# Turning k in VectorE's 32x32 blocks and through memory, not on TensorE, in an attention kernel on Trainium2

## The chip, the cores and the metric

The kernel runs on one core of one Trainium2 chip. The metric is the device time of one execution, in microseconds (us). Below, PE is TensorE (its weight loads have a row of their own, PEld), DVE is VectorE, ACT is ScalarE, POOL is GpSimd, and SP is SyncE, which issues all the DMAs of this kernel.

## The reference, cut to what matters

```python
x = x + attn(layernorm(x))          # x: 4 x 512 x 512; 32 query heads, 8 k/v heads, D = 128, chunks of 128 tokens
x = x + ffn(layernorm(x))

# attn, for each k/v head and batch; chunk n of four
q, k = rope(q), rope(k)
G = cumsum(g)                                                   # within a chunk
y_intra = ((q @ k.T) * causal(exp(G_i - G_j))) @ (v * dt)
cstates = einsum('jd,je->de', k * exp(G_last - G), v * dt)      # needs k with tokens on the rows
state   = state * exp(G_last) + cstates                         # over the chunks
y_inter = (q * exp(G)) @ state_before
y = rms_norm(y_intra + y_inter) * gnorm_w
y = y * (gate * sigmoid(gate))                                  # gate = x @ Wg.T
return y @ Wo.T
```

## The kernel before

Three stages follow one another: the first norm with v and the tables (to about 135 us of the trace), the attention stage (to about 1290 us), and the output projection with the second norm and the expert layer.

The attention stage is a sequence of 32 steps, one for each group `g` of four query heads (8) and each batch `b` (4), numbered `n = 4g + b`. Each step works through four chunks `c` of 128 tokens. Most groups run inside a hardware loop on each engine except PE, whose code is written out. Within a step PE does, in this order, for the chunks: `scores` (q times k, three passes over high and low parts), projections of the next step's k and q and of this step's gates (`next_unit`, `gates`; 12 matmuls each), `chunk_state` (the product `cstates`, three passes, into `p_cst`) for chunks 0 to 2, and `mix` (y from the state and from the probabilities). Nine projections share three PSUM banks in turn, so that a projection can begin only when VectorE has read what stood in its bank.

Each engine runs its own instructions in order, and semaphores join them. On VectorE the order in a step is: probabilities, scaled q, low part of the next chunk's q, `make_z` of the chunk before, a rope rotation (three instructions at L104 to L106), `turn_z` (z's 32x32 blocks), `make_state` (which empties `p_cst`, L972 and L975), `make_gate`. The rope's last addition is POOL's (L114).

The product `cstates` wants k with its tokens on the partitions, while the projection and the scores leave k with its head dimension there. `k_turn` therefore has PE transpose three chunks of the next step's k into PSUM bank `p_tok` (L805), between the last gate projection and `mix` of chunk 3. ACT copies `p_tok` rounded to the high part (`save_k`, L1120), VectorE takes the low part (`k_tok_low`, L929), and `chunk_state` of chunk 0 in the next step waits for both, and for `xw_low` of POOL (L1228).

Once in four steps weights are split too. In steps with b = 2 (of the groups 0 to 6) VectorE and POOL each take half of the low part of the next group's q weights (`q_low_weights`, L905, and `w_low`, L1241), just ahead of the step's end; in steps with b = 3 VectorE takes half of the gate weights' low part (L910) at the end, and POOL the other half at the start of the following step.

`make_tanh` (ACT, L1095) writes tanh of the gate's projection into a tile `tanh`, and waits until the gate before it has been made out of that tile; `make_gate` (VectorE, L935) makes `gate[c % 2]` of it.

SP issues, in a step: v for the next step, rows of the tables `g` and `e` (`load_g`, L663; `load_e`, L667), weights (L650, L657), and the stores of z (`store_z`, L752, four DMAs, for half 0 at c = 2 and for half 1 at c = 0 of the following step). The row of g for the next step's chunk 0 is issued at c = 1. POOL masks it (L1214) after it has copied a small table (L1206); both stand in POOL's queue ahead of the last rope addition.

## Time and profile before

| | |
|---|---|
| median of 3 runs | 1774.86 us (1773.87 to 1774.93) |
| the profiled execution's own time | 1773.33 us |
| its span, first to last instruction | 1771.5 us |
| mean granted TensorE clock | 0.996 |
| one attention step (four of them: 36.00, 35.90, 35.90, 35.90 us) | 35.9 us |
| PE, VectorE, ScalarE, GpSimd busy, share of the span | 98%, 72%, 40%, 48% |

The table's busy shares are averages over three stages. In the attention stage VectorE is far busier than its average, and PE is busy all the time. A busy PE says only that some matmul was under way by the trace's model; how closely they follow one another is read from their start times.

### The profile page before, as it was taken

The numbers are of one execution on the slowest core, as the hardware profiler recorded it, in microseconds if no ns is written. First come the engines' busy times: TensorE is split into PE (matmuls) and PEld (weight loads), VectorE is DVE, ScalarE is ACT, GpSimd is POOL, SyncE is SP. The second block draws the span as 40 slices with busy tenths as digits, with TensorE's granted clock in tenths as the row PEclk, the third lists the DMA queues.
The fourth block names the chain that finished last, engine by engine and source line by source line (L and its number), as shares of the span: only waits on it lengthen the run. The fifth ranks groups of instructions, "written<-read, shape, count | busy, mean of one in ns | idle before, by whom it ended". The sixth has DMA issues, their size and how long they took to land. (4 is left out here: it accounts for less than half of the span.)

```text
span 1771.5 us, 27984 instructions
## 1 busy us (share of the span) xinstructions
PE 1741.7 (98%) x8744; PEld 1469.5 (83%) x8744; DVE 1270.9 (72%) x2353; ACT 715.5 (40%) x2232; POOL 851.4 (48%) x862
## 2 busy tenths in 40 slices
PE   7998999999999999999999999999989999999998
PEld 6787888888888888888888888888878888888886
DVE  5326898988999999999898999998874333333332
ACT  3424444454445444544445444544652111111111
POOL 3225677667757766676766775776501101010101
PEclk9999999999999999999999999999999999999999
DMA  6333323423333333343342333333572323232321
GB/s 203 91 106 100 115 87 99 127 91 107 119 90 114 121 89 96 106 122 87 99 128 93 104 118 92 111 93 111 191 248 79 107 72 107 72 106 72 106 72 47
DMA packets 145985, 190.31 MB, mean 107 GB/s; under 512 B 9136, under 2 KB 79792, under 8 KB 145840
## 3 DMA queue, kind: packets, MB, share of 16 engines
q1 hardware_dynamic: 145840, 188.58, 34.8%
q8 instruction: 66, 1.08, 0.3%
q14 instruction: 79, 0.65, 0.1%
HBM read 141.89 MB, written 46.66 MB: 106 GB/s over the span
## 5 line engine op out<-in xcount | busy, mean ns | idle before, releaser
L114 POOL TENSOR_TENSOR q<-raw_wo_early 128x512 f32<-128x512 f32 x128 | 164.9, 1289 | 202.0 <-DVE raw_wo_early L106 201.5
L85 PE MATMUL p_proj<-shared,wq_hi 128*128 128x512 f32 x744 | 244.5, 390 | 0.0
L1113 ACT ACTIVATE square<-p_y 128x128 f32<-128x128 f32 x512 | 134.6, 278 | 216.4 <-PE p_y L837 216.0
L1846 POOL TENSOR_TENSOR var<-mv,eps 128x1 f32<-128x1 f32 x16 | 3.1, 192 | 403.9 <-DVE mv L1696 403.9
L837 PE MATMUL p_y<-v_tok,probs 128*128 128x128 f32 x1024 | 182.1, 275 | 0.0
L985 DVE SCALAR_TENSOR_TENSOR z<-p_y,srstd,gate 128x128 f32<-128x128 f32 x512 | 143.4, 341 | 48.9 <-issue 31.8
L1088 ACT ACTIVATE probs<-g_row,stab 128x128 f32<-128x128 f32 x512 | 164.3, 406 | 25.2 <-POOL g_row L1214 25.2
L85 PE MATMUL p_kept<-wg_hi,shared 128*128 128x512 f32 x560 | 173.2, 390 | 0.0
L1228 POOL TENSOR_TENSOR xw_lo<-xw_raw,xw_hi 128x512 fp32r<-128x512 f32 x96 | 131.1, 1365 | 86.6 <-ACT xw_hi L1125 86.6
L85 PEld LDWEIGHTS p_proj<-shared,wq_hi 128*128 128x128 f32 x744 | 139.6, 188 | 30.4 <-DVE raw_wo_early L106 1.2
L85 PE MATMUL p_proj<-wg_hi,shared 128*128 128x512 f32 x528 | 162.6, 389 | 0.0
L1236 POOL TENSOR_TENSOR srstd<-svar,mhalf 128x4 f32<-128x4 f32 x128 | 157.8, 1232 | 10.0
L837 PEld LDWEIGHTS p_y<-v_tok,probs 128*128 128x128 f32 x1024 | 150.0, 192 | 2.5
L836 PE MATMUL p_y<-state,qs 128*128 128x128 f32 x768 | 148.3, 275 | 1.4 <-DVE qs L950 1.4
L85 PE MATMUL p_proj<-shared,wq_lo 128*128 128x512 f32 x372 | 144.8, 389 | 0.0
L1378 DVE TENSOR_TENSOR wq_lo<-w_raw,wq_hi 128x1024 fp32r<-128x1024 f32 x62 | 75.8, 1223 | 84.3 <-ACT wq_hi L1373 84.3
L836 PEld LDWEIGHTS p_y<-state,qs 128*128 128x128 f32 x768 | 121.1, 191 | 7.1 <-issue 2.2
L1125 ACT ACTIVATE xw_hi<-xw_raw 128x512 fp32r<-128x512 f32 x96 | 60.7, 632 | 155.2 <-POOL xw_raw L1224 129.7
L85 PEld LDWEIGHTS p_kept<-wg_hi,shared 128*128 128x128 f32 x560 | 104.6, 188 | 21.5
L85 PEld LDWEIGHTS p_proj<-wg_hi,shared 128*128 128x128 f32 x528 | 99.1, 188 | 20.9
L1224 POOL TENSOR_TENSOR xw_raw<-v_tok,stab 128x512 f32<-128x512 f32 x96 | 111.3, 1159 | 0.1
L85 PE MATMUL p_kept<-wg_lo,shared 128*128 128x512 f32 x280 | 109.2, 390 | 0.0
(239 smaller groups left out, 4402.2 us busy)
## 6 DMA issues: line engine op xcount, KB each, us to landing
g_row<-g_scratch SPq DMA_DIRECT2D x128, 256.0 KB, 4.9
z_scratch<-z_st SPq DMA_DIRECT2D x256, 128.0 KB
w_raw<-z_scratch SPq DMA_DIRECT2D x62, 512.0 KB, 6.5
e_row<-e_scratch SPq DMA_DIRECT2D x96, 256.0 KB, 4.0
w_raw<-in_wq_t SPq DMA_DIRECT2D x16, 512.0 KB, 7.2
w_raw<-in_wg_t SPq DMA_DIRECT2D x16, 512.0 KB, 5.3
v_tok<-v_scratch SPq DMA_DIRECT2D x32, 256.0 KB, 2.9
v_scratch<-n_xin SPq DMA_DIRECT2D x22, 256.0 KB, 2.3
```

Source lines behind the costliest of these rows:

```text
L85: mm = pe.matmul(out, lhs[a], rhs[e], start=(i == 0 and j == 0), stop=(i == len(pairs) - 1 and j == 2))
L114: pool.tensor_tensor(out, keep["rope_a"][:, s, :], keep["rope_b"][:, s, :], ALU.add).then_inc(keep["roped"], 1)
L836: pe.matmul(p_y[c % 2][:, h, :], qs[:, h, :], state[:, c % 2, h, :], start=True, stop=False)
L837: mm = pe.matmul(p_y[c % 2][:, h, :], probs[:, c % 2, h, :], v_tok[:, b % 2, c, :], start=(c == 0), stop=True)
L985: zz = dve.scalar_tensor_tensor(z[:, h, :], p_y[c % 2][:, h, :], srstd[:, c, h:h + 1], gate[:, c % 2, h * D:(h + 1) * D], ALU.mult, ALU.mult)
L1088: e = act.activation(probs[:, c % 2, h, :], g_row[:, c % 2, h, :], ACT.Exp, bias=stab[:, b % 2, c, T_BIAS, h:h + 1])
L1113: s = act.activation(square[:, h, :], p_y[c % 2][:, h, :], ACT.Square, scale=2.0 / float(np.sqrt(D)), accum_out=ssum[:, c, h:h + 1])
L1125: act.activation(xw[0][:, :, :], xw_raw[:, :, :], ACT.Copy).then_inc(xw_hi_set, 1)
L1224: pool.tensor_tensor(xw_raw[:, :, :], v, w, ALU.mult).then_inc(xw_raw_set, 1)
L1228: pool.tensor_tensor(xw[1][:, :, :], xw_raw[:, :, :], xw[0][:, :, :].bitcast(F32), ALU.subtract).then_inc(xw_set, 1)
L1236: pool.tensor_tensor(srstd[:, c, :], svar[:, c, :], mhalf[:, :], ALU.pow).then_inc(srstd_set, 1)
L1378: dve.tensor_tensor(by_half(keep["z_lo"][slot]), raw_z(keep, raw_slot), by_half(keep["z_hi"][slot].bitcast(F32)), ALU.subtract).then_inc(k ...
```

## The change

Three things change in the attention stage; the other edits (one semaphore in the place of two or three, in the first and the last stage) leave instructions and waits as they were.

1. PE turns k only for the first step. For each later one VectorE transposes the 32x32 blocks of k in place of order (`turn_k`), after `turn_z` of chunk 0; SP stores them to memory in four DMAs (`store_k`, one for each 32 partitions), each block at its turned place, and loads them back (`load_turned`) with the tokens on the partitions, ahead of z's stores. High and low part are then made of this SBUF tile `k_turned`.
2. `k_tok_low` thus reads two SBUF tiles, where it read one of PSUM and one of SBUF.
3. tanh is written into the place of the gate that is made of it, and waits for z of two chunks before, not for the last gate.

```diff
+            def store_k(n):
+                sp.wait_ge(k_blocks_set, n)
+                for a in range(P // BL):
+                    sp.dma_start(k_dram.rearrange("c (b j) d -> j (c b) d", j=BL)[:, :, a * BL:(a + 1) * BL],
+                                 k_blocks[a * BL:(a + 1) * BL].rearrange("j c b i -> j (c b) i")).then_inc(k_out, 16)
+            def load_turned(n):
+                sp.wait_ge(k_out, 16 * (P // BL) * n)
+                sp.dma_start(k_turned[:, :, :], k_dram.rearrange("c t d -> t c d")).then_inc(k_in, 16)
@@ sync, step
                         load_e(g, b, 3)
+                        if ahead(n):
+                            store_k(n + 1)
                     elif c == 2 and ahead(n):
+                        load_turned(n + 1)
                         sp.wait_ge(state_set, 3 * n + 3)
@@ tensor
-            def k_turn(n, b):
-                pe.wait_ge(roped, ROPED * n + 1)
-                wait_ge(pe, tok_saved, n)
+            def first_k_turn():
+                pe.wait_ge(roped, 1)
                 for c in range(NC - 1):
-                    t = pe.transpose(p_tok[:, c, :], k[:, b % 2, c * C:(c + 1) * C], ident[:, :])
+                    t = pe.transpose(p_tok[:, c, :], k[:, 0, c * C:(c + 1) * C], ident[:, :])
                 t.then_inc(tok_done, 1)
@@ tensor, step
                 gates(g, b, n, 3)
-                k_turn(n + 1, b + 1)
                 mix(g, b, n, 3)
@@ vector
-                dve.tensor_tensor(k_tok[1][:, :, :], p_tok[:, 0:NC - 1, :], k_tok[0][:, :, :].bitcast(F32),
+                dve.tensor_tensor(k_tok[1][:, :, :], by_tokens(n), k_tok[0][:, :, :].bitcast(F32),
                                   ALU.subtract).then_inc(tok_saved, 1)
+            def turn_k(n, b):
+                dve.wait_ge(roped, ROPED * n + 1)
+                wait_ge(dve, k_out, 16 * (P // BL) * (n - 1))
+                dve.transpose(k_blocks[:, :, :, :], k[:, b % 2, 0:(NC - 1) * C].rearrange("p (c b i) -> p c b i", c=NC - 1, i=BL)
+                              ).then_inc(k_blocks_set, 1)
@@ vector, make_gate
-                dve.scalar_tensor_tensor(gate[:, c % 2, :], tanh[:, :], 1.0,
+                dve.scalar_tensor_tensor(gate[:, c % 2, :], gate[:, c % 2, :], 1.0,
@@ vector, step
                 turn_z(n, 0)
+                turn_k(n + 1, b + 1)
                 make_state(n, b, 1)
@@ scalar, make_tanh
-                wait_ge(act, gate_set, NC * n + c)
+                wait_ge(act, z_set, NC * n + c - 1)
@@ scalar
-            def save_k(n):
-                act.wait_ge(tok_done, n + 1)
+            def k_tok_high(n):
+                if has_last(n):
+                    act.wait_ge(k_in, 16 * n)
+                else:
+                    act.wait_ge(tok_done, 1)
                 wait_ge(act, cst_done, 3 * n)
-                act.activation(k_tok[0][:, :, :], p_tok[:, 0:NC - 1, :], ACT.Copy).then_inc(tok_hi_set, 1)
+                act.activation(k_tok[0][:, :, :], by_tokens(n), ACT.Copy).then_inc(tok_hi_set, 1)
```

`by_tokens(n)` is `k_turned` for all steps but the first, and `p_tok` for that.

On PE, at the end of a step (the last gate projection into `p_kept`, then `mix` of chunk 3), the rows before:

```order
 L85 MATMUL p_kept<-wg_hi,shared 128x512 x2
 L85 MATMUL p_kept<-wg_lo,shared 128x512
 L805 MATMUL p_tok<-ident,k 128x128 x3
 L836 MATMUL p_y<-state,qs 128x128
 L837 MATMUL p_y<-v_tok,probs 128x128
```

and after:

```order
 L85 MATMUL p_kept<-wg_hi,shared 128x512 x2
 L85 MATMUL p_kept<-wg_lo,shared 128x512
 L857 MATMUL p_y<-state,qs 128x128
 L858 MATMUL p_y<-v_tok,probs 128x128
```

The three transposes have gone from between them.

On VectorE, in the middle of a step (rope of the next step's second q head, z's blocks of chunk 0, the state of chunk 1, the gate of chunk 1), before:

```order
 L106 TENSOR_TENSOR raw_wo_early<-p_proj,raw_wo_early 64x512
 L994 STREAM_TRANSPOSE z_st<-z 128x16x32
 L975 SCALAR_TENSOR_TENSOR state<-state,e_row,p_cst 128x128 x4
 L935 SCALAR_TENSOR_TENSOR gate<-tanh,p_proj 128x512
 L943 TENSOR_TENSOR probs<-p_score,probs 128x512
```

and after:

```order
 L106 TENSOR_TENSOR raw_wo_early<-p_proj,raw_wo_early 64x512
 L1019 STREAM_TRANSPOSE z_st<-z 128x16x32
 L954 STREAM_TRANSPOSE k_blocks<-k 128x384
 L1000 SCALAR_TENSOR_TENSOR state<-state,e_row,p_cst 128x128 x4
 L960 SCALAR_TENSOR_TENSOR gate<-gate,p_proj 128x512
 L968 TENSOR_TENSOR probs<-p_score,probs 128x512
```

The transpose of k's blocks stands between z's and the making of the state.

On SP, in the first step's chunks 1 and 2 (row of e, weights of k for the next group, rows of g, row of e, half 0 of z), before:

```order
46 L667 DMA e_row<-e_scratch 128x512 [waits state_set]
47 L650 DMA w_raw<-in_wk_t 128x4x128
48 L663 DMA g_row<-g_scratch 128x512 [waits decay_set] x2
49 L667 DMA e_row<-e_scratch 128x512 [waits state_set]
50 L752 DMA z_scratch<-z_st 4x32x256 [waits turned]
```

and after:

```order
46 L686 DMA e_row<-e_scratch 128x512 [waits state_set]
47 L667 DMA k_scratch<-k_blocks 32x12x32 [waits k_blocks_set]
48 L667 DMA k_scratch<-k_blocks 32x12x32 x3
49 L657 DMA w_raw<-in_wk_t 128x4x128
50 L682 DMA g_row<-g_scratch 128x512 [waits decay_set] x2
51 L673 DMA k_turned<-k_scratch 128x3x128 [waits k_out]
52 L686 DMA e_row<-e_scratch 128x512 [waits state_set]
53 L774 DMA z_scratch<-z_st 4x32x256 [waits turned]
```

The four stores of k stand ahead of the weights and of g's rows, and the load that waits for them stands ahead of the row of e and of z.

## Rows read from the trace of the kernel before

**Rows 1.** The page, busy time and instructions of each engine
```profile
PE 1741.7 (98%) x8744; PEld 1469.5 (83%) x8744; DVE 1270.9 (72%) x2353; ACT 715.5 (40%) x2232; POOL 851.4 (48%) x862
```
**Rows 2.** Busy time of the engines in four steps (b = 0, 1, 2, 3)
```profile
core 0: us, PE busy (x) PEld busy (x) DVE busy (x) ACT busy (x) POOL busy (x), PEclk, DMA share, GB/s
431.80:467.80 36.00, 36.00 (x192) 30.65 (x190) 32.68 (x61) 17.67 (x63) 25.47 (x25) 1.00 0.35 102
539.60:575.50 35.90, 35.90 (x191) 30.70 (x190) 33.89 (x63) 16.70 (x62) 25.04 (x25) 1.00 0.37 118
```
**Rows 3.** Waits of PE's weight loads, 200 to 1250 us; PE itself has none
```profile
PEld p_proj L85 <- DVE raw_wo_early L106: 1.2, 6, 0.2
```
**Rows 4.** Timeline of PE at the end of a step (start, duration, engine, line, tiles)
```profile
501.42 0.39 PE L85 MATMUL p_kept<-wg_lo,shared 128*128 128x512 f32 x1
501.65 0.49 PE L805 MATMUL p_tok<-ident,k 128*128 128x128 f32 x3
501.98 0.39 PE L836 MATMUL p_y<-state,qs 128*128 128x128 f32 x2
```
**Rows 5.** VectorE at the end of a step with b = 2
```profile
533.50 1.30 DVE L950 TENSOR_TENSOR qs<-q,e_row 128x512 f32<-128x512 f32 x1
...
538.39 3.35 DVE L905 TENSOR_TENSOR wq_lo<-w_raw,wq_hi 128x1024 fp32r<-128x1024 f32 x1
541.66 0.70 DVE L994 STREAM_TRANSPOSE z_st<-z 128x512 f32<-128x512 f32 x1
542.29 0.51 DVE L929 TENSOR_TENSOR k_tok_lo<-p_tok,k_tok_hi 128x384 fp32r<-128x384 f32 x1
```
**Rows 6.** GpSimd beside it
```profile
532.94 1.31 POOL L114 TENSOR_TENSOR q<-raw_wo_early 128x512 f32<-128x512 f32 x1 [1.74 <-DVE raw_wo_early L106]
...
538.29 2.37 POOL L1241 TENSOR_TENSOR wq_lo<-w_raw,wq_hi 128x1024 fp32r<-128x1024 f32 x1
540.61 2.29 POOL L1228 TENSOR_TENSOR xw_lo<-xw_raw,xw_hi 128x512 fp32r<-128x512 f32 x1
```
**Rows 7.** PE in the step behind it (b = 3), where the state's product begins
```profile
542.88 0.40 PE L85 MATMUL p_proj<-shared,wk_hi 128*128 128x512 f32 x1
543.11 0.40 PE L85 MATMUL p_cst<-xw_hi,k_tok_hi 128*128 128x512 f32 x1
```
**Rows 8.** VectorE from the end of that step into one with b = 0
```profile
575.63 0.56 DVE L929 TENSOR_TENSOR k_tok_lo<-p_tok,k_tok_hi 128x384 fp32r<-128x384 f32 x1 [0.51 <-ACT k_tok_hi L1120]
...
582.74 1.13 DVE L985 SCALAR_TENSOR_TENSOR z<-p_y,srstd,gate 128x128 f32<-128x128 f32 x4 [1.33 <-POOL srstd L1236]
...
585.91 0.68 DVE L106 TENSOR_TENSOR raw_wo_early<-p_proj,raw_wo_early 64x512 f32<-64x512 f32 x1
...
596.10 0.71 DVE L994 STREAM_TRANSPOSE z_st<-z 128x512 f32<-128x512 f32 x1
596.74 1.08 DVE L975 SCALAR_TENSOR_TENSOR state<-state,e_row,p_cst 128x128 f32<-128x128 f32 x4
```
**Rows 9.** PE in that step: the q projection, and the state's product of chunk 2
```profile
586.74 0.41 PE L85 MATMUL p_proj<-shared,wq_hi 128*128 128x512 f32 x1
...
598.11 0.40 PE L85 MATMUL p_cst<-xw_hi,k_tok_hi 128*128 128x512 f32 x1
```
**Rows 10.** SP's issues in the step with b = 3
```profile
559.61 0.33 SPq L667 DMA_DIRECT2D e_row<-e_scratch  x1
560.12 0.90 SPq L657 DMA_DIRECT2D w_raw<-in_wg_t  x2
561.27 1.13 SPq L663 DMA_DIRECT2D g_row<-g_scratch  x2
...
567.33 2.85 SPq L752 DMA_DIRECT2D z_scratch<-z_st  x4
575.95 0.40 SPq L653 DMA_DIRECT2D v_tok<-v_scratch  x1
```
**Rows 11.** GpSimd there, where it meets the row of g
```profile
567.51 0.21 POOL L1206 COPY stab<-raw_wo_early 128x32 f32 x1 [1.12 <-DMA g_row<-g_scratch]
567.67 0.64 POOL L1214 TENSOR_SCALAR_AFFINE_SELECT g_row<-g_row 128x512 f32<-128x512 f32 x1
568.86 1.30 POOL L114 TENSOR_TENSOR q<-raw_wo_early 128x512 f32<-128x512 f32 x1 [0.55 <-DVE raw_wo_early L106]
```
**Rows 12.** The page, the DMA queue that SP fills
```profile
q1 hardware_dynamic: 145840, 188.58, 34.8%
```

43 lines of the change are left out of this document (23 added, 20 removed).

## The prediction, made before the changed kernel ran

> **What bounds the kernel now.** I read the page's engine line first, then the waits of PE, then busy time by steps, then the timelines of PE, VectorE and GpSimd at the two ends of a step. PE is busy for 98% of the span [rows 1], and between 200 and 1250 us nothing makes it wait but six weight loads, 1.2 us in all [rows 3]. So in the attention stage PE's own list of instructions is the time, and whatever leaves it should come off the end. But VectorE stands right behind it: 32.7 to 33.9 us busy in a step of 36 [rows 2]. That is 94% in a step with b = 3, and the second question is at which instructions PE just escapes waiting for VectorE. Between the two lists there are two such places, both in the groups where weights are split, and the change touches both.
>
> **Part 1, PE's transposes go.** The last gate matmul starts at 501.42, the transposes at 501.65, `mix` at 501.98 [rows 4]. The first distance, 0.23 us, is a matmul's pitch and stays; the transposes hold PE for 0.33 us. They stood in 31 steps (the first k is still turned on PE): 31 x 0.33 = 10.2 us off PE's list. That is the whole possible gain, 0.6%.
>
> **Part 2, what follows where nothing was left over.** Every other engine's work that starts from the last gate projection now has 0.33 us less until PE needs it, and VectorE has one instruction more.
>
> The added transpose of k's blocks: z's transpose of 512 columns at 596.10 is followed by the next instruction at 596.74, 0.64 us [rows 8]. With 384 columns, a quarter less, some 0.5 us (bounds 0.48 = 0.64 x 0.75, and 0.64). In steps with b = 1 and 2 it lies ahead of a wait of VectorE for PE and costs nothing; in b = 3 VectorE has 0.51 us of idle time before `k_tok_low` [rows 8], which takes it up. POOL wrote that k long before, so the transpose itself waits for nobody, and the state behind it is late only where VectorE has no pause.
>
> Place A, steps with b = 0 behind a weight split, n = 4, 8, ... 28, seven of them. VectorE's chain begins with z at 582.74, which waited for POOL's row statistics behind the weights' low part, and has no pause until the k rope's last instruction ends at 585.91 + 0.68 = 586.59 [rows 8]. PE's q projection, which needs that bank, starts at 586.74 [rows 9]. That is 0.15 us, and the six waits of [rows 3] are these: PE is bound by VectorE here already, and 0.15 is the time from the one to the other. PE coming 0.33 us sooner waits 0.33 us longer: the transpose that went in the step before is worth nothing. Then the state of chunk 1: it ends at 596.74 + 1.08 = 597.82 [rows 8] and PE's product of chunk 2, which needs `p_cst` emptied, starts at 598.11 [rows 9]. With 0.5 us more it ends at 598.32, and PE can start at 598.32 + 0.15 = 598.47: 0.36 us late. Together 0.33 + 0.36 = 0.69, seven times: 4.8 us.
>
> Place B, the start of steps with b = 3 (n = 3, 7, ... 27, seven). Here `k_tok_low` matters. VectorE and GpSimd hold each other up when both read SBUF twice: the scaled q, started at 533.50 next to POOL's addition of 532.94 to 534.25, took 1.30 us and ended 0.55 us after it, not 0.69 after its own start; the weight split started at 538.39, POOL's half ran from 538.29 to 540.66, and VectorE's ended at 541.74; and POOL's `xw_low`, started at 540.61, ended at 542.90, 1.16 us after that [rows 5, 6]. One runs, the other stands. `k_tok_low` at 542.29 did not stand (0.51 us beside that `xw_low` [rows 5]): it read PSUM. In the changed kernel it reads two SBUF tiles at the same moment, so it should stand until 542.90 and then need 0.4 us (0.55 for 512 columns, so 0.41 for 384): 543.31. PE starts the product at 543.11 [rows 7], now at 542.78; it will start at 543.31 + 0.15 = 543.46, so it loses 0.68 us. Seven times: 4.8 us. At the other starts of steps the two do not meet, or PE comes later.
>
> The Trainium skill, "SBUF — State Buffer", describes the same as an exclusive lock on a port pair that VectorE and GpSimd share: a VectorE instruction with two SBUF inputs meets a GpSimd one that reads SBUF, and the later one blocks for the whole of the earlier. By that page too the sum for place B is what the rows give, and by its rule PSUM as a source was worth having.
>
> **Part 3, SP's queue.** Four stores and a load go in. An issue took 0.40 us (v) to 0.71 us (z, 2.85 for four) [rows 10]; four stores of k, 1.6 to 2.9 us, say 1.9. They stand ahead of the weights and of g's row for the next step, and behind that row POOL waits, with the rope's last addition, row statistics and xw behind its wait. In the steps with b = 3 this is tight: g's row was issued at 561.27 behind a megabyte of gate weights [rows 10], and POOL waited for it until 567.51, 1.12 us [rows 11]. The stores bring 4 x 384 pieces of 128 B (the diff's patterns), 96 to each of the 16 DMA engines. No row shows the price of such a piece. By bytes the lot would be 0.5 us at some 400 GB/s; by pieces it would be 96 x 68 ns = 6.5 us, 68 ns being the queue's mean (0.348 x 1771.5 x 16 / 145840, [rows 12]) for pieces ten times as large. I take 1.3 to 2.5, nearer to the low end, since the pieces are small. So the row comes about 1.9 us late. What does that cost? The mask's end moves from 568.31 to 570.2, the rope's last addition from 568.86 to 570.2 [rows 11], 1.3 us; what POOL makes then is needed by z and by `k_tok_low`, which itself waited for ACT until 575.63 [rows 8]. By the rows' distances the first 1.9 us of delay are taken up. Cost 0; above 1.9, nearly one to one. The load back waits for the stores, lands by about 571 (my estimate from the issues above), and is needed at 575; z's stores behind it slip by about 2 us, and z's next transpose into the same half comes most of a step later.
>
> **Part 4, tanh.** It saves a wait that is not on PE's path; 0.
>
> **Sum.** 10.2 - 4.8 - 4.8 = 0.6 us gained, so 1772.7 against the profiled execution's own 1773.33. The median of the runs is 1.5 us above that execution; I forecast against the median, 1774.86 - 0.6 = **1774.3 us**.
>
> **Rivals.**
> - *Most of it arrives.* If `k_tok_low` does not stand behind `xw_low`, place B is bound by `xw_low` alone (542.90 to 543.11): about 0.15 us lost, not 0.68, and the sum is 10.2 - 4.8 - 1.1 = 4.3 off: 1770.6. For it: the order in which the two ask for SBUF may shift by tenths of a us. Against it: three collisions above, all the same way. Chance 0.16.
> - *All of it arrives.* PE's list decides alone, 10.2 off: 1764.7. It would take slack that rows 8 and 9 don't show. Chance 0.07.
> - *Slower: the stores hold up g's row in the b = 3 steps.* From 1.9 us of delay on POOL's chain, and through the weight split the next step's z and rope, run late. At 3.2 us (33 ns a piece, half the mean) it is 1.3 us x 7 = 9 us on top of the sum: 1783.4. For it: the DMA engines are full in just that stretch, and POOL waits there already [rows 11]. Against: DMA work in the other steps is light (share 0.35 [rows 2]). The Trainium skill, "DMA: Bandwidth & Descriptors", Specifications, says that pieces under 512 B are a read-modify-write; that speaks for this rival. Chance 0.20.
> - *The change does not do what it says* (PE still turning k): excluded by the order of PE's instructions.
> - The forecast itself, with both losses near their size: chance 0.57; its own range 1772 to 1777.
>
> **How the numbers follow.** About 0.2% (3.5 us) is what a measurement of this kernel can tell from no change. Faster by more than that: the first two rivals' 0.23, of which the first lies just beyond the bound, so 0.22 with some of the forecast's. Slower: 0.20, nearly all of the third. Same: 0.58. The range that leaves out the second rival and the tail of the third: 1769.5 to 1783.
>
> **What would show it.** Right: PE's waits, which had no row, now name `k_tok_low` (about 0.6 us, seven times) and the state of chunk 1 (0.3 to 0.4, seven times), the weight loads' wait for the rope grows from 0.2 to 0.5; steps with b = 1 and 2 are 35.6 us long and those with b = 0 and 3 about 36.3; `k_tok_low` lasts about 1.0 us at the start of b = 3. Wrong: if `k_tok_low` lasts 0.5 there, place B falls; if POOL waits for g's row for over 3 us, the third rival; if ACT waits for the load of k, a path that I hold to be slack.

## The result, and the profile of the changed kernel

The changed kernel takes **1781.76 us** (median of 6 runs, 1780.34 to 1784.88), the kernel before 1774.58 us beside it (6 runs, 1773.80 to 1775.14). The ratio is 1.0043, 95% interval 1.0032 to 1.0054. It is slower by 7.2 us; the forecast was 0.6 us faster, and the chance given to "slower" was 0.20. The profiled execution took 1780.34 us, its span is 1778.5. In both kernels the clock granted to TensorE is full in the attention steps (1.00 in the columns of stretches, here and in [rows 2]), so it has no part in this.

The page of the changed kernel, engine line and queues; against [rows 1, 12]:

```profile
PE 1735.9 (98%) x8651; PEld 1459.6 (82%) x8651; DVE 1285.1 (72%) x2384; ACT 716.5 (40%) x2232; POOL 849.3 (48%) x862
...
q1 hardware_dynamic: 207840, 200.78, 39.7%
q8 instruction: 65, 1.06, 0.3%
q14 instruction: 86, 0.70, 0.1%
```

PE has 93 instructions and 5.8 us less to do, as the change says, and the span is 7.0 us longer. So PE now waits. The last two lines are the engines' code: it comes through the same DMA engines as the data, in pieces of 8 and 16 KB (0.70 MB in 86, 1.06 MB in 65). The page of before has them too, and I had not looked at them:

```profile
q8 instruction: 66, 1.08, 0.3%
q14 instruction: 79, 0.65, 0.1%
```

They turn out to matter most.

Busy time in four steps of the changed kernel (a step with b = 1, one with b = 3, the step with b = 0 behind it, and the last step with b = 0; columns as in [rows 2]):

```profile
core 0: us, PE busy (x) PEld busy (x) DVE busy (x) ACT busy (x) POOL busy (x), PEclk, DMA share, GB/s
469.60:505.20 35.60, 35.60 (x189) 30.52 (x187) 32.91 (x67) 16.89 (x62) 24.18 (x26) 1.00 0.46 128
540.70:577.10 36.40, 35.89 (x189) 30.45 (x187) 34.97 (x64) 16.48 (x62) 25.68 (x25) 1.00 0.44 124
577.10:614.30 37.20, 36.08 (x187) 30.28 (x187) 32.30 (x61) 17.92 (x64) 24.66 (x24) 1.00 0.40 106
1155.80:1192.30 36.50, 36.16 (x189) 30.33 (x187) 33.90 (x62) 17.96 (x64) 25.63 (x25) 1.00 0.36 97
```

The lengths of all steps, from one first score product to the next, tell where the 7 us are:

| steps | how many | before | after | together |
|---|---|---|---|---|
| b = 1 and 2 | 16 | 35.90 | 35.55 | -5.7 |
| b = 3 (n = 3 to 27) | 7 | 35.92 | 36.41 | +3.5 |
| b = 0, n = 4 and 28 | 2 | 36.06, 35.93 | 36.43, 36.48 | +0.9 |
| b = 0, n = 8, 12, 16, 20, 24 | 5 | 35.99 | 37.96, then 37.23 to 37.26 | +7.0 |
| start and n = 0 | | | | -0.3 |
| the last step | 1 | 30.4 | 31.7 | +1.3 |
| output stage | | 483.0 | 483.4 | +0.4 |

The first three rows are what the prediction worked out. The fourth is not: five of the seven steps with b = 0 are 0.8 us longer still, and the first of them 1.5 us. These five have one thing in common that n = 4 and n = 28 lack: VectorE, ScalarE, GpSimd and SyncE reach them by a jump. Groups 1 to 6 are one loop on these engines. It is entered at n = 4 and left at n = 28 by running on, and it jumps back in front of n = 8, 12, 16, 20 and 24. I call them **jump steps** below.

Waits of PE, VectorE and ScalarE between 200 and 1250 us (us in total, times, the longest; before, PE had none [rows 3]):

```profile
PE p_proj L85 <- DVE raw_wo_early L106: 5.9, 7, 1.7
PE p_cst L85 <- POOL xw_lo L1258: 3.6, 7, 0.5
PE p_cst L85 <- DVE state L1000: 0.7, 4, 0.2
...
DVE q_lo L990 <- issue: 9.1, 5, 2.0
DVE probs L968 <- issue: 5.0, 4, 1.5
...
ACT square L1140 <- issue: 7.3, 5, 2.3
```

"Issue" is time in which an engine waited for nothing that the profile shows. In the kernel before these three came to 0.2 us for the squares, 0.9 for probs and nothing for q_lo. Five times is once for each jump step. VectorE at the start of n = 12, which begins at 577.07 (start, duration, idle time ahead):

```profile
577.56 0.56 DVE L947 TENSOR_TENSOR k_tok_lo<-k_turned,k_tok_hi 128x384 fp32r<-128x384 f32 x1
578.03 0.68 DVE L960 SCALAR_TENSOR_TENSOR gate<-gate,p_kept 128x512 f32<-128x512 f32 x1
578.63 1.87 DVE L928 TENSOR_TENSOR wg_lo<-w_raw,wg_hi 128x1024 fp32r<-128x1024 f32 x1
582.01 0.69 DVE L968 TENSOR_TENSOR probs<-p_score,probs 128x512 f32<-128x512 f32 x1 [1.51 <-issue]
584.61 0.96 DVE L990 TENSOR_TENSOR q_lo<-q,q_hi 128x512 fp32r<-128x512 f32 x1 [1.91 <-issue]
```

The same place in the kernel before, where the step begins at 575.51:

```profile
576.70 1.89 DVE L910 TENSOR_TENSOR wg_lo<-w_raw,wg_hi 128x1024 fp32r<-128x1024 f32 x1
578.75 0.69 DVE L943 TENSOR_TENSOR probs<-p_score,probs 128x512 f32<-128x512 f32 x1 [0.16 <-issue]
579.36 2.05 DVE L965 TENSOR_TENSOR q_lo<-q,q_hi 128x512 fp32r<-128x512 f32 x1
```

q_lo starts 3.9 us behind the step's start before and 7.5 us behind it after. z, the rope of k and PE's q projection stand behind it: place A of the prediction, with a cause it did not know. (Of the 1.4 us that a jump step has lost, 0.4 is the prediction's own: 0.69 at place A, less the 0.33 gained.)

The two places that the prediction did name. Place B, the start of a step with b = 3 (VectorE, GpSimd and PE; against [rows 5 to 7]):

```profile
543.78 1.03 DVE L947 TENSOR_TENSOR k_tok_lo<-k_turned,k_tok_hi 128x384 fp32r<-128x384 f32 x1
...
542.11 2.29 POOL L1258 TENSOR_TENSOR xw_lo<-xw_raw,xw_hi 128x512 fp32r<-128x512 f32 x1
...
544.91 0.47 PE L85 MATMUL p_cst<-xw_hi,k_tok_hi 128*128 128x512 f32 x1 [0.51 <-POOL xw_lo L1258]
```

`k_tok_lo` lasts 1.03 us in place of 0.51 and ends at 544.81, 0.41 us behind `xw_lo`; PE starts 0.10 us after it. The profile books PE's wait under `xw_lo`, which had ended 0.51 us before. And SyncE's queue with GpSimd's wait for g's row (against [rows 10, 11]):

```profile
562.09 0.33 SPq L686 DMA_DIRECT2D e_row<-e_scratch  x1
562.53 1.92 SPq L667 DMA_DIRECT2D k_scratch<-k_blocks  x4
564.62 0.92 SPq L676 DMA_DIRECT2D w_raw<-in_wg_t  x2
565.79 0.94 SPq L682 DMA_DIRECT2D g_row<-g_scratch  x2
566.85 0.38 SPq L673 DMA_DIRECT2D k_turned<-k_scratch  x1
569.28 0.33 SPq L686 DMA_DIRECT2D e_row<-e_scratch  x1
569.80 2.87 SPq L774 DMA_DIRECT2D z_scratch<-z_st  x4
...
571.13 0.21 POOL L1236 COPY stab<-raw_wo_early 128x32 f32 x1 [2.27 <-DMA g_row<-g_scratch]
```

The four stores took 1.92 us to issue (the prediction said 1.9), and g's row came 2.1 us later in relation to the next step's start than before (567.51 is 8.0 us ahead of 575.51, 571.13 is 5.9 ahead of 577.07), 2.5 us later counted from its own step's start, since the step is 0.4 longer.

### The profile page after: what moved, and what is told of

Same layout as the page of the kernel before. It is cut to its first block and busy times, and to the rows that moved or that the text cites. A ratio compares the mean times of both kernels' runs of the same rounds, so it can differ in the third digit from the quotient of the medians.

```text
span 1778.5 us, 28082 instructions
## 1 busy us (share of the span) xinstructions
PE 1735.9 (98%) x8651; PEld 1459.6 (82%) x8651; DVE 1285.1 (72%) x2384; ACT 716.5 (40%) x2232; POOL 849.3 (48%) x862
## 3 DMA queue, kind: packets, MB, share of 16 engines
q8 instruction: 65, 1.06, 0.3%
## 5 line engine op out<-in xcount | busy, mean ns | idle before, releaser
L1266 POOL TENSOR_TENSOR srstd<-svar,mhalf 128x4 f32<-128x4 f32 x128 | 154.1, 1204 | 10.0
```

What stands on the lines that cost most here:

```text
L1266: pool.tensor_tensor(srstd[:, c, :], svar[:, c, :], mhalf[:, :], ALU.pow).then_inc(srstd_set, 1)
```

## The experiments

The expectations speak of theories by number. Theory 1: k's stores make g's row late, with it GpSimd and ScalarE, and then the code at the jump is waited for. Theory 2: VectorE's own load. Theory 3: longer code as such. Theories 4 to 6 came with the results: z's stores in flight at the jump; the loads of the step's start; the place where a piece of code ends. Each run is given with its median, its ratio to the kernel before that ran beside it (1774.4 to 1775.7 us) with the 95% interval, and the mean length of its five jump steps. The medians are of all runs of a kernel; the lengths of steps are of the one execution that was traced, which is not always a typical one.

### Which part of the change: four runs

**e1**: VectorE writes its blocks straight into the tile that the load filled; no store, no load. The blocks stay where they are, so this is not the whole turn of k; it leaves out their change of places. (The edits below are cut to what matters.)

```diff
-                wait_ge(dve, k_out, 16 * (P // BL) * (n - 1))
-                dve.transpose(k_blocks[:, :, :, :], ...
+                dve.transpose(k_turned[:, :, :].rearrange("p c (b i) -> p c b i", i=BL), ...
-                    act.wait_ge(k_in, 16 * n)
+                    act.wait_ge(k_blocks_set, n)
-                            store_k(n + 1)  ...  load_turned(n + 1)
```

> The changed kernel, with VectorE's transpose written straight into k_turned and no store and no load of k (the blocks stay at their places, so the state's product is made of wrongly ordered k; all else is computed). In the changed kernel's trace steps with b = 1 and 2 take 35.55 us, b = 3 36.34, and b = 0 36.43 and 36.48 for n = 4 and 28, but 37.23 to 37.96 for n = 8 to 24, where the hardware loop jumps back. Theory 1 (the stores make g's row late, the row makes POOL and with it ACT late, and the code that both engines fetch at the jump is then waited for): the five steps fall to about 36.4 like the other two, the others stay; 1775 to 1776 us. Theory 2 (VectorE's own load, the transpose and the lock, costs it): nothing falls, 1781. Theory 3 (the longer code as such): half of the code that was added is gone, so at most half of the 0.8 us a step.

Measured: 1776.39 us, 1.0003 (0.9993 to 1.0012); jump steps 36.43, b = 3 36.34, b = 1 and 2 35.55. Without the transfers the change costs what the prediction's first two parts say together, nothing.

**e2**: PE turns k as before and tanh goes into the gate's place; the stores and the load are made, of tiles that nothing reads.

```diff
+                k_turn(n + 1, b + 1)        # TensorE, as before
-                turn_k(n + 1, b + 1)        # VectorE
```

> k turned by TensorE, and taken from PSUM, as in the kernel before; tanh in the gate's place; and the four stores and the load of k's size at the changed kernel's places on SP, of a constant tile and into one that nobody reads. Theory 1: steps with b = 1 and 2 at 35.90, b = 3 at 35.9 to 36.0, n = 8 to 24 about 0.9 above before's 36.0, so 1778 to 1780 us. Theory 2: as before, 1774.6 us, all steps at before's 35.9 to 36.0. Theory 3: in between, without a later row of g in POOL's waits.

Measured: 1776.68 us, 1.0007 (0.9997 to 1.0017); jump steps 36.37 (36.10 to 36.64), the others 35.90 as before. The transfers alone cost 1.9 us in the five jump steps of the trace, where Theory 1 wanted 0.9 in each, and 1.0 us by the medians. Neither half accounts for the 7 us. It also shows tanh in the gate's place to be worth nothing by itself, since the steps without a jump are as long as before.

**e3**: k's stores behind the next step's first row of g.

```diff
                             load_g(g + nb // B, nb % B, ncc)
+                        if cc == 2 and ahead(n):
+                            store_k(n + 1)
```

> The changed kernel with the four stores of k issued behind the row of g for the next step's chunk 0, not ahead of it (and behind the weights' loads); the load of the turned k stays where it is. Theory 1: POOL's wait for g's row falls from 24.8 us (18 times) to about before's 8.8 (7), n = 8 to 24 fall to about 36.4, 1776 to 1777 us. Theory 2 and 3: 1781 us, steps as they were.

Measured: 1794.14 us, 1.0103 (1.0086 to 1.0119); jump steps 39.67. GpSimd's wait for the row went back to 9.7 us in seven times, and the kernel lost another 12 us, where Theory 1 had forecast 1776 to 1777. That was a surprise: a late row of g alone is not the cause.

**e4**: VectorE's transpose of k behind the state and the gate of chunk 1.

```diff
                 turn_z(n, 0)
-                turn_k(n + 1, b + 1)
                 make_state(n, b, 1)
                 make_gate(g, b, n, 1)
+                turn_k(n + 1, b + 1)
```

> The changed kernel with VectorE's transpose of k behind make_state and make_gate of chunk 1, not ahead of them. If the transpose is what delays the state of chunk 1 at the steps with b = 0: the wait of p_cst for the state goes (0.7 us in 4), and n = 4 and 28 fall by up to 0.36 us, seven steps 2.5 us at most, 1779 to 1781. If those steps wait for the rope alone: no change, 1781.8. The stores come 1.6 us later, so by theory 1 the loop's steps may get longer by as much of it as the row of g is held up.

Measured: 1783.44 us, 1.0043 (1.0028 to 1.0058). n = 4 takes 36.26 us in place of 36.43, and n = 20 and 24 likewise 0.2 less, so the state's delay in place A is worth 0.17 to 0.2 us, half of what the prediction gave it. n = 8 fell by 0.75, n = 12 (37.82 us in place of 37.23) and n = 28 (36.94 in place of 36.48) grew, and the whole gained nothing; no run tells why.

### Theory 4, z's stores in flight at the jump

The trace of e3 suggested it: z's stores, 512 packets of 1,024 bytes and 46 ns, some 93 of them in a full microsecond, last some 6 us, and the later they end, the later ScalarE's squares start (z ends 0.4 us ahead of n = 12 before, 1.6 behind in the changed kernel, 4.9 behind in e3; squares at 1.5, 3.1, 6.0).

**e5**: before, with z's stores held.

```diff
                     elif c == 2:
+                        if ahead(n):
+                            sp.wait_ge(gate_set, NC * n + 4)
                         store_z(g, b, n, 0)
```

> The kernel before, with one wait added: SyncE holds the first half of z's stores of every step until the fourth gate is made, some 5 us later than the 8.3 us ahead of the next step's first score product at which it issues them now. Nothing else moves, and k is turned on TensorE. Theory 4, new after the first four runs: z's stores (512 packets of 1,024 bytes, some 4 under way at a time, 6.2 us long) should be over before the hardware loop jumps back, since the code that the engines fetch there stands behind them; where they end 0.5 us ahead of the step (before) ScalarE's squares start at 1.5 us, where they end 1.5 us behind it (after) at 3.0, and at 4.5 (k's stores behind g's row) at 5 to 6. By it this kernel, which has neither k's stores nor a late row of g, loses 1 to 3 us in each of the five steps into which the loop jumps (n = 8, 12, 16, 20, 24) and nothing in the 26 others, though z's stores are as late there: 1781 to 1790 us. Theory 1 (g's row late, and with it GpSimd and ScalarE) expects the time of the kernel before, 1775, since g's row isn't moved at a step's start.

Measured: 1841.33 us, 1.0381 (1.0366 to 1.0396); jump steps 36.67, and it did not make the state of things that I wanted. SyncE was held until behind the jump (z issued 1.4 us behind n = 12, v 5.0 behind), so z was not in flight at the jump, and the rows of g and e came late in every group: GpSimd waited 118.6 us for g. Its 67 us tell nothing of theories 1 or 4. With the loads of the step's start 4.5 us late, the jump step n = 12 takes 35.93, which suggested Theory 5; the other four take 36.27 to 37.68.

**e6**: the changed kernel, z's stores cut by 32 partitions and not by blocks of columns; same bytes, same packets.

```diff
-                for j in range(TB):
-                    tiles = z_dram[b * TB:(b + 1) * TB, half, j * BL:(j + 1) * BL, bass.ds(g * HG, HG), :]
-                    sp.dma_start(tiles.rearrange("i a h t -> i a (h t)"), z_st[:, half, j]...)
+                for i in range(TB):
+                    tiles = z_dram[b * TB + i, half, :, bass.ds(g * HG, HG), :]
+                    sp.dma_start(tiles.rearrange("(j a) h t -> a j (h t)", a=BL), z_st[i * BL:(i + 1) * BL, half]...)
```

> The changed kernel, with z's four stores cut another way: one for each 32 partitions and all four blocks of columns, in place of one for each block of columns and all 128 partitions. Same bytes, same packets of 1,024 bytes, same place in SyncE's queue; the outer dimension has 32 entries in place of 4. If the four packets under way at a time come from that outer 4, z's stores take 2 to 3 us in place of 6.2 and end about 3 us ahead of the jump. Theory 4 then expects the five steps with the jump back at 36.4 us in place of 37.2 to 38.0, as without k's stores, and 1776 us. Theory 1 expects no change, 1781.8, since g's row, the stores of k and SyncE's times stay where they are. If the stores take 6 us as before, the run tells nothing of the theories.

Measured: 1774.27 us, 1.0003 (0.9995 to 1.0012). z's stores take 3.1 us in place of some 6 and end 1.1 to 2.0 us ahead of the jump steps; the jump steps take 37.27 us all the same (one of them 36.17, the others 37.22 to 37.99). So Theory 4 falls for the changed kernel. The gain of 7.5 us by the medians comes at the end: in the trace the output stage, which reads z back, takes 480.0 us in place of 483.4, and the last step 28.7 in place of 31.7.

**e7**: the same cut in the kernel before.

> The kernel before with z's stores cut by partitions as in the run above. There they end 0.5 us ahead of the jump, and ScalarE's squares start when its own work is done, so that Theory 4 expects no gain or a small one: 1774 to 1775.5 us, steps with the jump 35.9 to 36.0. It shows what the new cut is worth by itself.

Measured: **1768.75 us, 0.9965** (0.9952 to 0.9978); all steps as before, again with the gain behind them. I had looked for it in the jump steps and expected nothing.

**e8**: e6, and k by tokens earlier.

```diff
+                    k_tok_high(n + 1)       # ScalarE, right behind q_high(n + 1, ...)
...
                 if group_ahead(g) and b == B - 2:
+                    k_tok_low(n + 1)        # VectorE
                     q_low_weights(g + 1)
```

> The changed kernel with z's stores cut by partitions, and the two halves of k by tokens made earlier: ScalarE writes k_tok_hi right behind the next step's first q_hi in every step (k comes from memory now and needs no turn on TensorE), VectorE writes k_tok_lo ahead of its 3.4 us on wq's low half in the steps b = 2, so that it no longer reads two SBUF tiles beside GpSimd's xw_lo. If the 1.03 us of k_tok_lo and its place behind xw_lo are what makes the steps b = 3 take 36.3 us, these fall to 35.6, by 0.75 x 7 = 5 us; with the run above that gives 1771 us, and 1770 to 1774 with what it does elsewhere. If the lock has nothing to do with it, b = 3 stays at 36.3 and the time is that of the run above.

Measured: 1778.81 us, 1.0034 (1.0021 to 1.0047). Four steps with b = 3 take 35.63 to 35.87 us (the expectation of e11 miscounts them as three) and PE's wait in front of the state's product is gone: it begins 3.50 us into the step, as before (3.52), in place of 4.17. `xw_lo` starts where it did, 1.39 us into the step, and ends at 3.00 in place of 3.66, so both of the things that PE waits for came earlier; that `k_tok_lo` is the later of the two is shown by the changed kernel's times above. The expectation of 1770 to 1774 failed. The other three took 37.7, and n = 4 and n = 28 took 37.5 and 37.4 in place of 36.8 and 36.3: more lost than gained.

### Theory 5, the loads of the step's start

**e9**: the changed kernel, with SyncE's first three loads of a step held in b = 0.

```diff
                     if has_last(n):
+                        if b == 0:
+                            sp.wait_ge(q_lo_set, NC * n + 2)
                         sp.wait_ge(y_done, NC * n)
```

> The changed kernel with one wait added: in the steps b = 0 SyncE holds the loads of the step's start (v, a row of g, a row of e: 512 KB and more, under way from 1.5 to 5.5 us behind the step's start) until VectorE has made q_lo of the second chunk. Theory 4 in its first form fell: with z's stores spread they end 1.5 us ahead of the step and the jump steps still take 37.2 us. Theory 5: the code that VectorE fetches next stands behind those loads. In the kernel before, VectorE branches 0.21 us behind the step's start and ScalarE 1.17 ahead of it, and q_lo follows its probs without a wait; in the changed one they branch at 0.58 and at 0.09 (right behind xw_raw, which waits for g's row), a fetch is made at 5.5, once the loads are through, and q_lo starts at 7.5; z, the turn of k and TensorE's wq unit follow it, the last 1.1 us late. By Theory 5 q_lo starts at 5 us or less, the steps n = 8 to 24 take 36.4 us in place of 37.2 to 38.0, as without k's stores, and the whole 1776.5 to 1778. By Theory 3 (the code is just longer or lies otherwise) or if ScalarE's late branch alone counts (0.1 us late is 1 us), the steps stay at 37.2 and the time at 1781.8.

Measured: 1777.98 us, 1.0020 (1.0011 to 1.0029); jump steps 36.72, 37.25, 36.16, 36.37, 36.43. Four of five came back to 36.2 to 36.7; q_lo's waits fell from 9.1 to 6.3 us and did not go, and at n = 12 q_lo starts at 7.2 us where 5 or less was expected.

**e10**: e9 with e6's cut. **e11**: and k by tokens early, in b = 2 alone. **e12**: the kernel before with the loads held and the cut.

> The changed kernel with the loads held as above and z's four stores cut by 32 partitions. The cut alone gave 1774.3, all of it behind the 31st step (5 to 7 us less in the last step and the output stage) and none in the jump steps. If the two don't meet, the 4.5 us of the jump steps come off that: 1769.5 to 1771. By Theory 3 1774.3.

> As the run above, and in the steps b = 2 ScalarE's k_tok_hi goes right behind q_hi and VectorE's k_tok_lo ahead of its part of wq (in the others both stay in place). In the run with this in every step, the steps b = 3 took 35.63 to 35.87 in three of seven and 37.7 in the other four, where the jump at their end was late; the wait of the state product for xw_lo and k_tok_lo at 4.2 us was gone. With the loads held, 35.6 in all seven: 0.72 x 7 = 5 us less, 1765. If the jump at the end of b = 3 has a loss of its own, one or more of them stay at 37.7 and the time is 1770 or more.

> The kernel before with the loads held and z's stores cut by 32 partitions. Its jump steps have 0.1 us to lose, so Theory 5 expects what the cut alone gave, 1768.7 (1767.5 to 1769.5); the held loads themselves cost something if this is above 1770. It is the measure for the run above: is k turned on VectorE worth having, once its side effects are gone?

Measured: e10 1771.59 us, 0.9982 (0.9973 to 0.9991), jump steps 36.25; e11 1776.94, 1.0012 (1.0003 to 1.0021), 37.31; e12 **1768.09, 0.9966** (0.9954 to 0.9978), 35.97. Theory 5 holds as far as it goes. e11, forecast at 1765, missed by 12 us: it did shorten b = 3 (four of seven at 35.62 to 35.83), and n = 4 and n = 28, which see no jump, grew from 36.46 and 36.29 to 37.11 and 37.36.

**e13**: e11 with e3's order. **e14**: e3's order with e6's cut. **e15**: e10 with e3's order.

> The changed kernel with all of it: k's stores behind g's first row, the loads of the step's start held in b = 0, z's stores cut by 32 partitions, and the halves of k by tokens early in b = 2. In the run without the first of these the jump steps took 37.3 to 37.6 us, with xw_raw ending 1.2 to 1.4 us behind the step's start (0.5 ahead of it where g's row is on time) and ScalarE's branch 0.1 behind that. Theory 1: g's row is late because k's stores stand ahead of it, and with it on time xw_raw ends at -0.5, the jump steps take 36.0 to 36.5 us, 1768 to 1771 in all. If the 3 us that k's stores behind g's row cost in each jump step by themselves (1794 us in all) are there again, 1790.

> The kernel with k's stores behind g's first row, which took 1794.1 us (jump steps 39.4 to 40.0), and z's stores cut by 32 partitions; the loads aren't held. In it ScalarE branched on time (0.5 us ahead of the step), but its next code came 4.8 to 6.2 us later in place of 2.4 to 2.9, with z's stores under way until 4.5 us behind the step's start. Theory 4, for this kernel: the stores of z did it; spread they end 1 to 2 us behind the step's start at the latest, the code comes after 2.4 to 3.5 us and the jump steps take 36.4 to 37.3: 1771 to 1776. If it was something else in that order (SyncE late, k's load), the jump steps stay near 39.5 and the time at 1787.

> As the first run of these, without the early halves of k: it stands beside the run with k's stores in place, the loads held and z's stores spread (1771.6 us; jump steps 36.0 to 36.9, xw_raw's end at 0.0 to 0.75). Theory 1: g's row on time takes another 0 to 0.5 us from each jump step, 1769 to 1771.5, for with the loads held most of what the late branch costs is hidden.

Measured: e13 1770.96 us, 0.9984 (0.9975 to 0.9993); e14 1773.90, 0.9998 (0.9989 to 1.0007); e15 1769.97, 0.9976 (0.9966 to 0.9986).

- e14 against e3: 39.67 fell to 37.25 in the jump steps. In e3, with z's stores in flight until 4.9 us behind the step's start, ScalarE's next code came 6.2 us behind its branch, in e14 2.5. For e3 Theory 4 was right. ScalarE there and in e14, at the start of n = 12 (578.86 and 576.98):

```profile
579.74 1.06 ACT L1105 ACTIVATE wg_hi<-w_raw 128x1024 fp32r<-128x1024 f32 x1
584.84 0.28 ACT L1140 ACTIVATE square<-p_y 128x128 f32<-128x128 f32 x1 [4.05 <-issue]
```

```profile
577.85 1.05 ACT L1105 ACTIVATE wg_hi<-w_raw 128x1024 fp32r<-128x1024 f32 x1
579.20 0.28 ACT L1140 ACTIVATE square<-p_y 128x128 f32<-128x128 f32 x1 [0.29 <-issue]
```

- e15 against e10: g's row on time is worth 0.1 us in a jump step (36.16, 36.25), and 1.6 us in all by the medians, with intervals that overlap.
- e13 against e15: b = 3 takes 35.64 in place of 36.33 in all seven, by 4.8 us together, and the steps with b = 0 behind them take 36.99 to 37.21 (one 36.64) in place of 35.95 to 36.47. e13's jump steps were forecast at 36.0 to 36.5 and took 37.04. What PE gains at the start of b = 3 it waits for one step later, 0.67 and 0.68 us in n = 4 and n = 28 too, which see no jump. From the start of n = 27 VectorE in e13 pauses once in 43 us, 0.97 us ahead of one z (in e15 another 0.80 us ahead of `k_tok_lo`), so the two places are nearly one bound.

### Theory 6, where a piece of code ends

In e14 nothing was left of theories 1 and 4, and q_lo still waited 10.8 us in five times (VectorE at n = 12, which begins at 576.98):

```profile
580.91 0.69 DVE L968 TENSOR_TENSOR probs<-p_score,probs 128x512 f32<-128x512 f32 x1 [0.49 <-issue]
583.95 1.55 DVE L990 TENSOR_TENSOR q_lo<-q,q_hi 128x512 fp32r<-128x512 f32 x1 [2.35 <-issue]
```

The trace's records of VectorE's register instructions show that its sequencer itself stood still there, between probs and the register work for q_lo. Counting the 64-byte instructions in the compiled programs, the loop's code begins at number 438 in the kernel before, 442 in e1, 445 in the changed kernel (the traces hold as many records more: 4 from before to e1, 3 from e1 to e17, 5 from e14 to e18). The stop is 3 instructions into the loop, so at 448. If a piece of code ends there, in e1 it ends behind q_lo and one more instruction, and in the kernel before among the instructions of z. VectorE waits for GpSimd's row statistics there anyway: in e1 its next record comes 0.03 to 0.05 us behind their end in all five jump steps. So these two kernels show no stop for code at 448; they only leave room for one that costs nothing.

**e16**: the changed kernel, ten waits for a semaphore long set ahead of VectorE's loop (loop at 450). **e17**: e1 with five of them (loop at 445). **e18**: e14 with ten (450).

```diff
                 dve.memset(eps4[:, :], 4.0 * EPS).then_inc(const_set, 1)
+                for _ in range(10):          # e17: 5
+                    dve.wait_ge(const_set, 2)
```

> The changed kernel, with ten waits of VectorE for a semaphore that has long been set, ahead of the loop: five more instructions of 64 bytes in front of the loop's code, nothing else. Theory 6: an engine fetches its code in pieces of 8,192 bytes, 128 instructions. By the count of instructions in the programs VectorE's loop begins at instruction 445 in the changed kernel, 442 without k's stores, 438 before. In the changed one VectorE's sequencer stops between probs and the register work for q_lo, 3 instructions into the loop: 448, which is 3.5 x 128. At 442 the same boundary falls behind q_lo (VectorE waits for row statistics there anyway), and at 438 within z. So the piece with q_lo is asked for only when VectorE has come to it, and its fetch stands behind the loads of the step's start. With the loop at 450 the boundary lies ahead of it. Theory 6 expects q_lo without its wait (9.1 us in five steps now), the jump steps at 36.2 to 36.7 in place of 37.2 to 38.0, and 1776.5 to 1778.5 in all, though every transfer and g's row stay as they are. Theory 5 alone (only what stands in the DMA queues counts) and Theory 1 (g's row) expect 37.2 to 38.0 and 1781.8.

> The reverse: the kernel without k's stores and load (VectorE's blocks written straight to k_turned; 1776.4 us, jump steps 36.43), with five such waits ahead of the loop, three more instructions, so that VectorE's loop begins at 445 as in the changed kernel. Theory 6 expects the loss without a single added transfer: q_lo waits 2 us in each jump step and these take 37.0 to 37.4 us, 1779.5 to 1781. Theories 1 and 5, for which k's transfers are the cause, expect no change: 36.43 and 1776.4.

> The kernel with k's stores behind g's first row and z's stores cut by 32 partitions (1773.9 us; jump steps 37.25, though ScalarE branches on time, g's row is on time and z's stores are over; q_lo waits 10.8 us in five steps), and ten such waits ahead of the loop. Theory 6 expects jump steps at 36.0 to 36.45 and 1769 to 1770.5, as with the loads held (1770.0). If something else keeps them at 37.25, it stays at 1774.

Measured: e16 1779.59 us, 1.0032 (1.0020 to 1.0045), 2.2 us below the changed kernel; e17 **1783.12, 1.0048** (1.0034 to 1.0062), 6.7 us above e1; e18 1773.39, 0.9990 (0.9981 to 0.9999), 0.5 us below e14. VectorE at n = 12 in e1 (step from 575.51) and in e17 (from 577.37):

```profile
580.01 0.69 DVE L964 TENSOR_TENSOR probs<-p_score,probs 128x512 f32<-128x512 f32 x1 [1.07 <-issue]
580.62 1.15 DVE L986 TENSOR_TENSOR q_lo<-q,q_hi 128x512 fp32r<-128x512 f32 x1
583.11 1.13 DVE L1006 SCALAR_TENSOR_TENSOR z<-p_y,srstd,gate 128x128 f32<-128x128 f32 x4 [1.35 <-POOL srstd L1262]
```

```profile
583.39 0.69 DVE L966 TENSOR_TENSOR probs<-p_score,probs 128x512 f32<-128x512 f32 x1 [2.58 <-ACT probs L1112]
585.77 0.69 DVE L988 TENSOR_TENSOR q_lo<-q,q_hi 128x512 fp32r<-128x512 f32 x1 [1.68 <-issue]
```

And in e16 (from 576.76), with all transfers of the changed kernel:

```profile
581.90 0.69 DVE L970 TENSOR_TENSOR probs<-p_score,probs 128x512 f32<-128x512 f32 x1 [1.70 <-issue]
582.51 0.68 DVE L992 TENSOR_TENSOR q_lo<-q,q_hi 128x512 fp32r<-128x512 f32 x1
584.25 1.12 DVE L1012 SCALAR_TENSOR_TENSOR z<-p_y,srstd,gate 128x128 f32<-128x128 f32 x4 [1.06 <-POOL srstd L1268]
```

The pieces of code themselves are on the pages. Queue 14 of e1, of e17 and of e16:

```profile
q14 instruction: 79, 0.65, 0.1%
q14 instruction: 84, 0.69, 0.1%
q14 instruction: 81, 0.66, 0.2%
```

e17 fetches five pieces of 8 KB more than e1, and e16 five fewer than the changed kernel (86), as e18 does against e14 (81, 86): one for each jump.

All at n = 12. Branch and q_lo's start are in us from the step's start; "code after" is the time from the branch to the engine's next register instruction, from the trace's records; jump steps: mean of five.

| kernel | loop at | ScalarE branches, code after | VectorE branches, code after | q_lo starts | jump steps |
|---|---|---|---|---|---|
| before | 438 | -1.2, 2.4 | 0.2, 2.8 | 3.9 | 35.99 |
| e1 no transfers | 442 | -0.5, 2.8 | 0.6, 3.7 | 5.1 | 36.43 |
| e17 the same | 445 | -0.5, 2.6 | 0.9, 4.9 | 8.4 | 37.65 |
| changed | 445 | 0.1, 2.9 | 0.6, 4.2 | 7.5 | 37.39 |
| e16 the same | 450 | 0.1, 2.7 | 0.6, 4.4 | 5.8 | 36.59 |
| e3 | 445 | -0.5, 6.2 | 0.6, 5.2 | 8.9 | 39.67 |
| e14 | 445 | -0.5, 2.5 | 0.6, 3.2 | 7.0 | 37.25 |
| e18 the same | 450 | -0.5, 2.8 | 0.6, 2.9 | 4.3 | 36.39 |
| e15 e14, loads held | 445 | -0.5, 2.7 | 0.6, 3.1 | 6.1 | 36.16 |

Theory 6's place of the code is borne out. e17 makes the loss, 6.7 us by the medians and far outside the intervals, where not one of the change's transfers exists; theories 1 and 5 expected nothing there. The waits in front of q_lo and the one more piece at each jump come and go together: with the loop at 450 neither e16 nor e18 has such a wait, and the jump steps take 36.33 to 36.42 us in four of five (e16; n = 8 kept 37.37, where g's row comes later and ScalarE branches at 0.9, in the changed kernel too) and 36.39 to 36.41 in all five (e18).

Three things don't fit so well. e17 lost more than the 37.0 to 37.4 us a step and 1779.5 to 1781 in all that were expected: in its five jump steps VectorE's first code too comes later, 4.7 to 4.9 us behind the branch where e1 has 3.3 to 3.7, and a piece that ends further on gives no reason for that. With the loop at 450 most steps with b = 3 take 36.48 us in place of 36.34, without a cause that I know. And the medians give back less than the traces. e16's is 1 us above the 1776.5 to 1778.5 expected and 2.2 below the changed kernel's, where the jump steps of the two traces differ by 4.0; four of its six runs are faster than the changed kernel's fastest, but the intervals of the ratios overlap. e18's median is 3 us above its 1769 to 1770.5, and 0.5 us from e14's, where the jump steps differ by 4.3. Of e14's eleven runs the traced one is the slowest (1777.07), of e18's the fastest (1770.78), so that pair shows the wait and the pieces, and no gain in time.

## Why the prediction was wrong, by its own steps

**Part 1** (0.33 us from each step): right. b = 1 and 2 take 35.55 us, 0.35 less, 5.7 us in 16 steps.

**Part 2.** The transpose lasts 0.54 us, in the range of 0.48 to 0.64.

*Place A*, 0.69 us a step: in e1, where nothing else disturbs it, a step with b = 0 takes 36.31 to 36.46 us, against 35.93 to 36.06 less 0.35: 0.73 to 0.82 lost. Of its two terms the weight loads' wait for the rope went from 0.2 to 0.6 us at most (e1: 3.9 us in seven times), the state's delay is 0.17 to 0.2 by e4 and not 0.36. So the total came out near, and its split was off.

*Place B*, 0.68 us: `k_tok_lo` lasted 1.03 us where 1.0 was forecast, and the steps take 36.34 us, so 0.77 is lost; taking `k_tok_lo` out of the way (e13) gives 0.69 back. The Trainium skill, "SBUF — State Buffer", "SBUF: two separate sides", has VectorE and GpSimd exclude one another where both need the shared port; by that, the trace agrees, here again and in e13, where `k_tok_lo` beside GpSimd's weight split took 2.70 us:

```profile
536.68 2.70 DVE L949 TENSOR_TENSOR k_tok_lo<-k_turned,k_tok_hi 128x384 fp32r<-128x384 f32 x1
...
536.58 2.38 POOL L1276 TENSOR_TENSOR wq_lo<-w_raw,wq_hi 128x1024 fp32r<-128x1024 f32 x1
```

That the two losses add was right too, in e1. What the prediction did not see is that they can't be cured one by one: e13 cured place B and gave it back at place A. (Its first rival has a slip: with `xw_lo` alone PE would start at 542.90 + 0.15, so 0.27 us late and not 0.15, and the time would be 1771.4. Nothing else hangs on it.)

So parts 1 and 2, together 0.6 us faster, stand within the noise: e1 measured 1776.39 against 1775.7 beside it, 0.7 more, and a ratio that can't be told from 1.

**Part 3 and the sum** are where it failed: "Cost 0" for SyncE's queue, and no term at all for the engines' code at the loop's jump. The terms of part 3 were near (issue 1.92 us, said 1.9; the row 2.5 us late, said 1.9; packets of 128 bytes took 13 ns each, so 96 on each engine some 1.25 us, said 1.3 to 2.5). The transfers' cost was not 0, though small by themselves: 1.0 us by e2's medians, 1.9 in its jump steps. The larger part was looked for nowhere. From e1 to the changed kernel the jump steps went from 36.43 to 37.39, 4.8 us in five, and what decides in them is when VectorE's and ScalarE's code arrives. The prediction treated the added step on VectorE as one instruction of 0.5 us. Three of them alone cost 6.7 us in e17. No line of the prediction concerns this: it is a term put at nothing without a reason, and not a mis-sized one.

**Part 4** (tanh, 0): e2 agrees.

**The third rival** had the right side and almost the number (1783.4) for the wrong reason. It said that g's row, over 3 us late, holds up GpSimd in the steps b = 3. GpSimd did wait up to 3.3 us in some steps (24.8 us in 18), which by the prediction's own test would have confirmed it. But e14, with the row on time, stays at 37.25 in the jump steps, and e15 against e10 puts the row's worth at 0.1 us a jump step. That the time came near this rival's is luck. z's slow stores, which the prediction let slip by 2 us at no price, are harmless to the changed kernel's jump steps (e6) and harmful in e3.

**What stays open.** In the trace of the changed kernel the jump steps are 7.0 us longer, b = 3 and the other b = 0 steps 4.4, less 5.7; the last step's 1.3 us and the 0.4 of the output stage were not taken apart. Of the jump steps' 1.40 us each, e16 gives 0.80 to the place of the code, e1 shows 0.44 without any of it, and the 0.16 that are left are not assigned. By the medians the place of the code is worth 2.2 of the 7.2 us, and e16 is still 4.3 us further above the kernel before than e1 is; how much of this is the transfers, no pair of runs tells. Why e1 gains nothing in the median though its steps end level with the kernel before (its last step begins at 1258.29, before 1258.08) while its later stages take 2.6 us more, no run tells. Nor could the addresses at which the code lies in memory be seen. That a piece ends at 448 is inferred from one stop; the shifts from 442 to 445 and from 445 to 450 bear it out, and 448 is 3.5 times the 128 instructions of an 8 KB piece, so the half is unexplained.

**A version that beats both.** The kernel before with z's stores cut by partitions (e7), 1768.75 us, or with the loads held as well (e12), 1768.09 us, 0.3% below the kernel before; the two can't be told apart. The best of the changed kernel's versions (e15) reaches 1769.97, with q_lo still waiting 8.0 us in five times; e15 with its code moved was not run. As far as measured, turning k on VectorE is not worth having: against e12, e15 wins 1.2 us up to the last step (1256.82 against 1258.05) and loses 3.1 behind it.

## What to carry to other kernels

Where engines run a loop, look at the steps behind its jump by themselves, and at idle time booked as "issue" in them: added instructions on an engine move where its pieces of code end, and a piece that ends just ahead of an instruction on the path costs a fetch at every jump: here some 2 us of wait, 0.8 to 1.2 us of the step in the traces. A handful of waits that wait for nothing, ahead of the loop, tests this in one run, with the count of instruction pieces on the page as the sign. Judge what it is worth by the medians, since one trace may be of the slowest or the fastest run. When an edit takes a wait from one place of a chain nearly without gaps, ask at which place the same chain is waited for next. And a store whose outer dimension has 4 entries may keep a quarter of the DMA engines busy (z's did, by 4.3 packets at a time): check how many of its packets are under way at once.

## What the runs showed of the hardware that I had not expected

- **Code comes by DMA, behind data.** After the jump back at n = 12 the next register instruction of ScalarE came 2.4 to 2.9 us behind the branch, and 6.2 us with z's stores in flight (e3); VectorE's 2.8 to 3.2 us in the kernel before, e14, e15 and e18, and 3.7 to 5.2 in the others of the table, of which e17 (4.9) has no transfer that e1 (3.7) lacks. A second piece, fetched while the step's loads were under way, cost q_lo up to 3.5 us of wait (e6), and up to 1.8 with the loads held (e10). The Trainium skill, "Runtime: NRT & Kernel Launch", Instruction fetch mechanics, says that a taken branch out of the pages at hand forces a fetch; by that, the trace agrees. It also says that a boundary costs little and is mostly hidden, which the measured 2 us in front of q_lo do not bear out right behind a jump.
- **A DMA's shape sets how many of its packets are under way.** z's stores with 4 entries in the outer dimension had some 93 packets of 46 ns under way in each full microsecond, so 4.3 at a time, and took 6.0 to 6.3 us for 512 KB; with 32 entries the same packets took 2.3 to 3.1 us. That was worth 5.7 us by the medians in the kernel before (e7) and 7.5 in the changed one (e6), at the end of the kernel:

```profile
z_scratch<-z_st SPq DMA_DIRECT2D x256, 128.0 KB, 2.5
```

  (the page of e7: from issue to landing 2.5 us, where the pages of before and after give none).
- **Packets of 128 bytes are cheap here**: 13 ns each in the changed kernel's trace, where those of 2,048 bytes took 84 ns by the median and 120 on average in the attention stage; the stores land 2.6 us after their issue (median of 124 on the page).
